# Cross attention: the split Q and K rows spread over the partitions in four groups of four heads instead of two of eight

## The reference

```python
q = x @ w_q + b_q
k = context @ w_k + b_k
v = context @ w_v + b_v
q = q.reshape(B, Lq, N_HEADS, HEAD)
k = k.reshape(B, -1, N_HEADS, HEAD)
v = v.reshape(B, -1, N_HEADS, HEAD)
scores = jnp.einsum('bqhd,bkhd->bhqk', q, k) * scale
weights = jax.nn.softmax(scores, axis=-1)
out = jnp.einsum('bhqk,bkhd->bqhd', weights, v).reshape(B, Lq, D)
return out @ w_o + b_o
```

## Time and profile before

| | us |
|---|---|
| median of 3 runs | 4919.64 |
| lowest and highest of them | 4889.11, 4920.73 |
| the profiled execution itself | 4899.48 |
| its span, first to last instruction | 4897.7 |

### The profile page before, as it was taken

How to read it: one execution, slowest core, us unless ns; L and a number is a source line. 1 busy time by engine, 2 the same in 40 slices (tenths; PEclk the granted TensorE clock), 3 DMA queues, 4 the chain that set the end, 5 groups by cost and what they waited for, 6 DMA issues and landing times. The chain is left out here.

```text
span 4897.7 us, 120993 instructions
## 1 busy us (share of the span) xinstructions
PE 4476.6 (91%) x37859; PEld 2276.7 (46%) x37859; DVE 3087.1 (63%) x4487; ACT 2783.1 (57%) x5359; POOL 1707.7 (35%) x5154
## 2 busy tenths in 40 slices
PE   6999599999999999999599684999999999999997
PEld 3444344444444444444366472444444444444445
DVE  4555476666676666667444695766666666666662
ACT  4555266666666666667233431766666666666673
POOL 5555433333333333332166103433333333333310
PEclk9999798999998899989799796989999899998998
DMA  2111111111111111111000001111111111111110
GB/s 61 41 40 42 51 51 43 43 43 50 49 53 43 45 57 44 43 43 37 20 0 0 1 0 50 43 43 51 58 43 53 51 43 43 43 43 43 44 35 22
DMA packets 197159, 196.93 MB, mean 40 GB/s; under 512 B 67719, under 2 KB 159101, under 8 KB 196621
## 3 DMA queue, kind: packets, MB, share of 16 engines
q1 hardware_dynamic: 196620, 189.82, 13.4%
HBM read 25.59 MB, written 2.10 MB: 6 GB/s over the span
## 5 line engine op out<-in xcount | busy, mean ns | idle before, releaser
L709 ACT ACTIVATE cross_Pr<-cross_sT 128x512 f32<-128x512 f32 (+1 forms) x3584 | 1993.4, 569 | 1152.0 <-PE cross_sT L617 1072.2
L784 DVE TENSOR_REDUCE cross_nm<-cross_ring 128x1 f32<-128x802 f32 x2048 | 2031.9, 993 | 935.4 <-PE cross_ring L584 917.4
L617 PE MATMUL cross_sT<-cross_Q,cross_K 99*128 99x256 bf16 (+1 forms) x6656 | 1410.8, 289 | 88.0 <-issue 86.3
L637 PE MATMUL cross_oT<-cross_Pr,cross_V 128*32 128x256 f32 (+1 forms) x16384 | 1201.7, 365 | 0.3 <-ACT cross_Pr L709 0.3
L584 PE MATMUL cross_ring<-cross_K,cross_Q 72*128 72x401 bf16 x4096 | 1096.5, 350 | 64.4 <-DMA cross_K<-cross_kparts 62.1
L617 PEld LDWEIGHTS cross_sT<-cross_Q,cross_K 99*128 99x128 bf16 (+1 forms) x6656 | 484.3, 101 | 1079.4 <-ACT cross_Pr L709 506.7
L498 POOL TENSOR_TENSOR cross_mp<-cross_nm,cross_one 128x2 bf16<-128x2 f32 x512 | 101.1, 198 | 2089.8 <-DVE cross_nm L790 2089.8
L637 PEld LDWEIGHTS cross_oT<-cross_Pr,cross_V 128*32 128x32 f32 (+1 forms) x16384 | 334.2, 110 | 516.0 <-issue 422.4
L584 PEld LDWEIGHTS cross_ring<-cross_K,cross_Q 72*128 72x128 bf16 x4096 | 424.5, 109 | 145.7 <-issue 86.0
L696 ACT ACTIVATE cross_Q<-cross_pm 3x256 bf16<-3x256 bf16 x512 | 190.8, 373 | 180.1 <-PE cross_pm L603 173.2
L793 DVE TENSOR_REDUCE self_nm<-self_ring 128x2 f32<-128x512 f32 x256 | 174.4, 687 | 168.4 <-PE self_ring L589 115.1
(11 more groups left out here) (322 smaller groups left out, 4812.6 us busy)
## 6 DMA issues: line engine op xcount, KB each, us to landing
cross_K<-cross_kparts SPq DMA_DIRECT2D x576, 200.1 KB
cross_C<-in_ctx_dram SPq DMA_DIRECT2D x32, 576.0 KB
cross_Q<-cross_qparts SPq DMA_DIRECT2D x576, 32.0 KB
self_Q<-self_qparts SPq DMA_DIRECT2D x144, 64.0 KB
self_K<-self_kparts SPq DMA_DIRECT2D x144, 64.0 KB
cross_xs<-X SPq DMA_DIRECT2D x32, 128.0 KB, 2.1
X<-in_x_dram SPq DMA_DIRECT2D x4, 512.0 KB, 6.1
self_xs<-X SPq DMA_DIRECT2D x16, 128.0 KB, 2.1
```

The costliest lines, as they stand in the source:

```text
L617: mm = pe.matmul(sT[0:r, e[1] % 2, (c % 2) * S:(c % 2 + 1) * S], K[0:KROWS, h, s:s + r], Q[0:KROWS, h, :], start=True, stop=True)
L637: mm = pe.matmul(oT[32 * q:32 * q + 32, s:s + w], V32[0:r, h % cfg.keep, c, :], Pr[0:r, slot, (c % 2) * S + s:(c % 2) * S + s + w], start= ...
L709: act.activation(Pr[0:r, g % cfg.npr, 0:nchunk * S], sT[0:r, g % 2, 0:nchunk * S], ACT.Exp).then_inc(exped, 1)
L784: dve.tensor_reduce(nm4[:, sl, t, half:half + 1], R.rearrange("p (j n) -> p j n", j=2)[:, :, 0:cfg.block], AX.XY, ALU.max, negate=True).th ...
```

## The change

`GROUPS` goes from 2 to 4 for the cross attentions: a group is four heads in 32 partitions, its K piece [8 partitions, 4 heads, 1601]. The loop on SP stacks four groups and waits for `scored` after each quarter of the heads. All that is sized by groups follows: four `stacked` semaphores, PE waits for one every four heads, `SPLIT_Q` waits for four, `bq` comes in four DMAs, the weight columns are put in the other order.

```diff
-        self.groups, self.bufs = (2, 1) if self.cross else (1, 2)
+        self.groups, self.bufs = (4, 1) if self.cross else (1, 2)
...
             if cfg.cross:
                 load_ctx(1)
-                stack(1)
+                for g in range(1, GROUPS):
+                    stack(g)
...
                 if cfg.cross:
-                    sp.wait_ge(scored, NB * i + NB // 2)
-                    stack(0)
-                    sp.wait_ge(scored, NB * i + NB)
-                    stack(1)
+                    for g in range(GROUPS):
+                        sp.wait_ge(scored, NB * i + NB * (g + 1) // GROUPS)
+                        stack(g)
...
-GROUPS = 2
+GROUPS = 4
```

## The result

The changed kernel takes 5000.35 us (median of 4 runs, 4975.86 to 5034.64) where the one before takes 4908.18 (median of 4, 4889.11 to 4920.73). The ratio is 1.0196 with an interval of [1.0119, 1.0273]: slower by some 92 us. The forecast was 4915 with a range of 4880 to 4955, so the time lies outside it.

The account below looks back on a forecast made before the run. PE, busy 91% of the span, was taken as the bound, losing time only to idle and low clock. Per block -4.2 + 4.6 + 7, twice, gave +15 on 4899.48: 4915 us, range 4880 to 4955.

Parts of the forecast that it names:

- what the idle does to the clock: In each cross attention block's first batch, PE's 4.6 us idle costs 7 us through low clock, bounds 0 and 13.
- The prologue: At each cross attention block's start, group 0 lands 5.6 us earlier, bias DMAs add 1.4: PE starts 4.2 us earlier.
- The first batch: In each block's first batch, POOL's SPLIT_Q waits for all four groups, 10.6 us late; PE then stands 4.6 us.
- The loop: In the loop's batches the last group lands 16 us after the jump, 13 us before SPLIT_Q needs it: nothing late.
- A: In the first batches POOL's wait is short and the clock holds: 10 us less, 4889 us; chance 0.25.
- B: On SyncE smaller pieces cost as much as large ones, 1.16 us; PE waits 15.7 us per first batch: 4960; chance 0.1.
- C: At the loop's jumps code fetch meets stack traffic; 26 jumps add 13 to 26 us: 4935 us; chance 0.2.
- D: Only the block's start changes and low stretches fall elsewhere: scatter of 4889 to 4921 us, inside the forecast; no separate chance.

Follow-up runs that it names:

- The runs with bursts: Changed kernel plus unused matmuls in slot 42 of each block's first batch: 16 f32, 4915.5 us (10 runs); 64 bf16, 5024.84 us (one run).
- the idle late in the batch: Kernel before, with 14 POOL memsets ahead of head 14's value operation in the first batch of each cross attention block: 4987.19 us, one run.
- The later splits: Changed kernel with the first batch's Q and K splits for the next batch moved to later slots: 4899.95 us, ratio 0.9952 to the kernel before.
- the two with early fills: Kernel before, with POOL memsets ahead of the first batch's Q split: 14 memsets, 4984.47 us; 10 memsets, 4961.62 us; one run each.

## Why the prediction was wrong

**The step that failed** is one term: "I take 7 for each block, bounds 0 and 13", for what the idle does to the clock. It was sized by the low stretches behind two jumps, 23 and 10 us, on the ground that an idle "in the middle of busy work should do the same". Both stretches of the changed kernel were 119.5 us, and each cost some 52 us. The mechanism was named and its place was right; the length was carried over from another place in the batch. Behind a jump the f32 steps come soon: in the kernel before, at the first jump of the earlier trace rows, the output's projection ran from 941 and the transposes of the next context from 944, and the clock was back at 952. PE's MT of head 5 comes after the last of a batch's early f32 steps:

```profile
642.34 1.19 PE L563 MATMUL cross_ring<-cross_cT,cross_wk 97*128 97x512 f32 x4
```

That is the changed kernel's second K projection. It ends 1.6 us before PE goes idle and 6 us before MT. What follows are heads alone, with 32-column matmuls among them, until the V projections at 737. The runs with bursts show that dense work placed there ends the low stretch, and the idle late in the batch shows that the length depends on where in the batch the idle falls. What brings the clock back behind a jump, those f32 steps or something else, was not tried by itself; in the changed kernel the 16 and the 10 f32 matmuls of the V projections did not (below). That a busy PE does not bring it back at once could be read in the earlier trace rows: both stretches there count as fully busy at 0.50.

The Trainium skill ("TensorE: Matmul & The Clock Gate", section "HAM oscillation — how this bites in real kernels") puts the penalty at half the time spent throttled. The 0.44 measured here nearly agrees, and where they differ the measurement decides; it was not the factor that was wrong but the time spent.

**The sum as it came out.** 2 x 52 for the stretches, +9 for PE's two stalls, +9 for the jumps' idle (95.4 for 86.3), -12 for the earlier starts: 110. The two spans are 112.9 us apart, but that the sum comes so near is in part luck. By part of the program the changed kernel is 8.7 us longer ahead of the first cross attention block, where nothing was changed, 68 us longer in the first block and 36 in the second. The rest of the low stretches is scatter that differs by part: leaving out the two long ones, the first block has 27 us more at the low clock than before and the second 46 us less.

**The prologue held.** PE's start came 14.7 us after the stacking began, 15.1 said. Its two parts missed in opposite directions: the issue took 12.9 us (12.6 said), and the landing behind it 1.8, less than the lower bound of 1.9 (2.5 said). K pieces issue with a median of 0.67 us (0.71 with the gap to the next), 0.75 said. Here is the tile:

```profile
L394 SPq DMA_DIRECT2D cross_K<-cross_kparts x1152: 665/670/2212, 596.3 to 4813.3; - x192
```

Two small sizes were off: a Q piece went from 0.65 to 0.72 (6.51 us for 9) though its data halved, and `bq` cost 1.55 us more, above its bound of 1.4. From the block's first weight load to PE's first A the gain was 4.7 and 6.9 us, 11.6 in all; 8.4 was said (twice 4.2).

**The first batch held.** POOL late by 10.33 and 10.75 us (10.6 said), PE idle for 4.35 and 4.76 (4.6 said).

**The loop held.** Neither PE nor POOL waited for a stack there. The group that now crosses the jump is issued at the new pace, and it doesn't lengthen the low stretches: those behind the 26 jumps add up to 482 us now and to 485 before.

```profile
864.97 6.50 SPq L394 DMA_DIRECT2D cross_K<-cross_kparts  x9
871.59 6.39 SPq L394 DMA_DIRECT2D cross_Q<-cross_qparts  x9
```

**The rivals.** A, the gain stands, fell with the result. The later splits make it of the change, 24 us below the kernel before where A said 10 below; but A counted on a clock that holds by itself. B fell: the median K piece took 0.67 us, not 1.16. Its remark that the trace disagrees with the rule on small transfers was a weak reading, since pieces of 32 and 64 KB that issue in the same 0.65 us are what a fixed cost looks like. And B at 4960 is by itself more than 1% slower, so its chance of 0.1 and the 0.06 for all that is slower by over 1% do not fit together. C, the fetch meets the traffic, fell as a cause: the jumps' idle was 9.1 us more, and 87.8 in the run with the same traffic and later splits. D fell with the result; its remark on scatter was right, and bigger than thought: the kernel before ranged from 4886.7 to 4961.29 in the later runs. One of its sources is seen, a low stretch of 58 to 61 us at a jump, none to two of them in an execution; how much of the scatter it makes was not worked out. The changed kernel's profile has one:

```profile
2208.00:2269.00 61.00, 58.36 (x299) 24.89 (x299) 25.36 (x37) 21.38 (x41) 11.10 (x33) 0.50 0.07 24
```

**What would have served.** Bounds of the clock term from the code as well as from the rows: an idle that falls where the next f32 step is some 90 us off has the whole rest of the batch, over 100 us, as its upper bound. At half the length lost, 2 x 50 us would have been a rival with a chance of its own.

## What to carry to other kernels

Price an idle of TensorE by what runs behind it, not by its length: 4.4 us cost 52 more where some 90 us of heads followed, and dense matmuls put there cut the low stretch to 14 to 21 us. Before a buffer is filled by more, smaller transfers, look for the one instruction that waits for the last of them and for what stands behind it in its queue; moving that instruction, a two-line edit, turned 2% slower into 0.5% faster. And a loop jump that idles TensorE for 3.3 us costs 11 to 12 here; seven batches in a loop body were worth 5.4%, more than any staging tried here.

## What the runs showed of the hardware that was not expected

- Low clock with PE busy without a gap behind the idle can last: 92 to 119.5 us in five stretches of three kernels. Bursts of 16 f32 or 64 bf16 matmuls with 128 columns ended it within 4 to 6 us of their start, in four of four stretches. In the unaided kernels it came back at different steps: in the first blocks of the two with early fills it was back within 2 us of the end of the first V projection (16 f32 matmuls), in the changed kernel not before 767, past both V projections and before the next batch's first transposes (769.60):

```profile
737.63 3.62 PE L570 MATMUL cross_ring<-cross_wv,cross_cT 97*128 97x128 f32 x16
...
750.82 2.34 PE L570 MATMUL cross_ring<-cross_wv,cross_cT 97*128 97x128 f32 x10
```

  So what exactly makes it return isn't settled.
- An idle of 2.12 us dropped the clock once and once not, in one execution.
- A Q piece of half the size did not issue faster but slower: 0.72 us for 16 KB against 0.65 for 32 KB.
- The jump's idle goes with the jump, not with the data: 26 gave 86.3 us, 2 gave 6.6. The Trainium skill ("Runtime: NRT & Kernel Launch", section "Instruction fetch mechanics") says that a taken branch outside the current pages forces a fetch before the engine can go on, with no duration; the rows fit that, at 3.3 us each, but they show only that PE stood at the jump and not what it waited for.

Not tried: four groups with seven batches a jump, a projection moved for good into the heads-only stretch, and a burst with no idle ahead of it.
